# Graph attention layer on one core: the first stage's engine queues and transfers in another order

## The reference, cut to what matters

```python
h0 = maximum(layernorm(x), 0)
h  = h0 @ W.T + b_W
e  = (h @ a1)[:, None] + (h @ a2)[None, :] + b_a       # 4096 x 4096
e  = where(e > 0, e, 0.2 * e)
attention = softmax(where(adj > 0, e, -9e15), axis=1)
out = x + attention @ h
```

## Time and profile before

| | |
|---|---|
| time, median of 3 runs | 202.73 us (201.75 to 202.74) |
| span of the profiled execution, first to last instruction | 200.8 us |
| TensorE (PE) busy | 194.9 us, 97% |
| VectorE (DVE) busy | 183.0 us, 91% |
| ScalarE (ACT) busy | 147.9 us, 74% |
| GpSimd (POOL) busy | 52.4 us, 26% |
| read from memory | 73.08 MB |

### The profile page before, as it was taken

How to read it: one execution, slowest core, us unless ns; L and a number is a source line. 1 busy time by engine, 2 the same in 40 slices (tenths; PEclk the granted TensorE clock), 3 DMA queues, 4 the chain that set the end, 5 groups by cost and what they waited for, 6 DMA issues and landing times.

```text
span 200.8 us, 7230 instructions
## 1 busy us (share of the span) xinstructions
PE 194.9 (97%) x3183; PEld 189.2 (94%) x3183; DVE 183.0 (91%) x265; ACT 147.9 (74%) x192; POOL 52.4 (26%) x66
## 2 busy tenths in 40 slices
PE   7969999999999999999999999999999999999993
PEld 7648889999999999999999999999999999999993
DVE  4779999999998799897999999999999999999745
ACT  2679879898882777689988888899588888996000
POOL 1002479699995010205000000072000000510000
PEclk9999999999999999999999999999999999999999
DMA  5999999999999999999999999999999999997012
GB/s 181 376 417 418 407 403 423 421 418 415 422 432 408 418 423 419 416 421 418 415 419 423 419 418 421 421 411 421 419 418 418 415 421 416 418 383 226 6 43 66
DMA packets 15968, 75.66 MB, mean 377 GB/s; under 512 B 1600, under 2 KB 5952, under 8 KB 7616
## 3 DMA queue, kind: packets, MB, share of 16 engines
q1 hardware_dynamic: 15792, 75.06, 91.7%
q10 hardware_dynamic: 144, 0.13, 0.3%
HBM read 73.08 MB, written 2.11 MB: 374 GB/s over the span
## 4 chain that ended last, share of the span: by engine, by line
PE 91%; DMA 4%; SPq 1%; DVE 1%; issue 1%; POOL 0%
PE ps L836 29%; PE ps L834 29%; PE ps L840 29%; DMA adj_sb<-in_adj_t 4%; PE ps L808 2%; PE ps L798 2%; SPq L268 1%; SPq L273 1%; PE ps L876 1%; DVE mask L476 0%; POOL bad L788 0%; DVE rden L504 0%; DVE rg L510 0%; DVE bad L519 0%; DVE upper L576 0%
## 5 line engine op out<-in xcount | busy, mean ns | idle before, releaser
L834 PE MATMUL ps<-V,w 128*128 128x129 f16 x1024 | 174.3, 221 | 0.0
L836 PE MATMUL ps<-V,w 128*128 128x129 f16 x1024 | 174.3, 221 | 0.0
L840 PE MATMUL ps<-V,w 128*128 128x129 f16 x1024 | 174.3, 221 | 0.0
L379 ACT ACTIVATE mask<-adj_sb 128x1024 bf16<-128x1024 int32 x126 | 125.5, 1056 | 28.6 <-DMA adj_sb<-in_adj_t 28.6
L459 DVE SCALAR_TENSOR_TENSOR w<-g_row,pairs,mask 128x1024 f32<-128x1024 f32 x96 | 120.5, 1320 | 5.5 <-ACT mask L379 3.6
L834 PEld LDWEIGHTS ps<-V,w 128*128 128x128 f16 x1024 | 100.2, 98 | 1.5 <-ACT H L340 0.7
L836 PEld LDWEIGHTS ps<-V,w 128*128 128x128 f16 x1024 | 100.2, 98 | 1.0 <-issue 1.0
L840 PEld LDWEIGHTS ps<-V,w 128*128 128x128 f16 x1024 | 100.2, 98 | 0.0
L459 DVE SCALAR_TENSOR_TENSOR w<-ps,pairs,mask 128x1024 f32<-128x1024 f32 x31 | 37.4, 1267 | 0.0
L785 POOL TENSOR_TENSOR xT<-xT,x_sb 128x512 f32<-128x512 f32 x6 | 11.5, 1932 | 79.8 <-ACT xT L394 79.8
L739 POOL TENSOR_TENSOR x_sb<-x_sb,b_row 128x512 f32<-128x512 f32 x8 | 10.0, 1301 | 0.0
(11 more groups left out here) (93 smaller groups left out, 63.8 us busy)
## 6 DMA issues: line engine op xcount, KB each, us to landing
adj_sb<-in_adj_t SPq DMA_DIRECT2D x64, 1024.0 KB, 10.3
xT<-in_x_t SPq DMA_DIRECT2D x8, 256.0 KB, 7.5
x_sb<-in_x_p SPq DMA_DIRECT2D x3, 512.0 KB, 10.9
g_row<-g_dram SPq DMA_DIRECT2D x1, 1536.0 KB, 10.3
out<-xT SPq DMA_DIRECT2D x3, 512.0 KB, 9.9
x_sb<-in_x_p SPq DMA_DIRECT2D x2, 256.0 KB, 4.2
out<-xT SPq DMA_DIRECT2D x1, 192.0 KB, 3.4
out<-xT SPq DMA_DIRECT2D x3, 64.0 KB, 1.6
```

Of the source, the lines that this page charges most:

```text
L379: nc.scalar.activation(mask[:, m % MASKS, r], adj_sb[:, m % HELD, r], ACT.Relu, scale=CONNECTED).then_inc(mask_ready, 1)
L834: nc.tensor.matmul(sums[:, bank, a, :], w16[:, m % SLOTS, col:col + P, 1], V[:, jt, 0, 0:NF], start=(jt == 0 and a == 0), stop=False, skip ...
L836: nc.tensor.matmul(sums[:, bank, a, :], w16[:, m % SLOTS, col:col + P, 1], V[:, jt, 1, 0:NF], start=False, stop=False, skip_group_check=True)
L840: last = nc.tensor.matmul(sums[:, bank, a, :], w16[:, m % SLOTS, col:col + P, 0], V[:, jt, 0, 0:NF], start=False, stop=(jt == NT - 1), ski ...
```

## The change: what it does

- Scores of part 0 come straight from PSUM (`first_scores`), not from `H`; so they don't wait for `take_chunk`, and `take_chunk(0)` and `(1)` wait for them. Chunk 1 of h goes to PSUM banks 4 and 5, and the sum for `norm` to bank 7.
- The table load for the exponential stands ahead of `take_chunk(0)`, not behind `take_chunk(1)`; the two multiplications for `cc` stand behind `h_chunk(1)` and VectorE's `cc` steps behind the maximum of the scores.
- SP loads x's first set ahead of chunk 1 of the transposed x, and the first `adj` pair in two halves, with a semaphore of its own for the first half, ahead of chunks 2 and 3 and of x's third set.
- The low parts of chunk 0 are made by GpSimd (`first_lows`), and both parts of chunk 1 too (`halves(1)`). They stand ahead of `deviations(2, 3)` in its queue. VectorE's `products` and `lows` and ScalarE's `highs(1)` go away.
- On TensorE `h_chunk(2)` stands behind the row vector's transposes, and step 0 (`first_pair`) ahead of `h_chunk(3)` and `centre_chunk(4)`. Step 0 multiplies first what the high parts allow, then the low parts of its first side, then the second side. The chunks that stood behind step m now stand behind step m + 1.
- VectorE does x's third set's statistics in one go, behind step 0.

```diff
-    H_BANK = (1, 4, 1, 4, 4, 4, 4, 4)
+    H_BANK = (1, 4, 4, 4, 4, 4, 4, 4)
...
                 load_xt(0)
+                load_x(0)
                 load_xt(1)
-                load_x(0)
                 load_x(1)
+                sp.dma_start(adj_sb[:, 0, 0:GC], adj_t[0, :, 0:GC]).then_inc(adj_begun, 16)
                 load_xt(2)
+                load_xt(3)
+                sp.dma_start(adj_sb[:, 0, GC:2 * GC], adj_t[0, :, GC:2 * GC]).then_inc(adj_loaded[0], 16)
                 load_x(2)
-                load_xt(3)
-                load_adj(0)
+                load_adj(1)
                 load_xt(4)
-                load_adj(1)
...
                 def take_chunk(c):
                     act.wait_ge(h_done, c + 1)
+                    if c < 2:
+                        act.wait_ge(scores_ready, 1)
...
                 roots_part()
+                nc.scalar.activation(warm[:], zero_col[:], ACT.Exp)
                 take_chunk(0)
+                weights(0)
                 take_chunk(1)
-                nc.scalar.activation(warm[:], zero_col[:], ACT.Exp)
                 relu_chunk(2)
-                weights(0)
-                relu_chunk(3)
                 highs(0)
                 first_mask()
+                relu_chunk(3)
                 take_chunk(2)
                 mask_part(1)
                 take_chunk(3)
                 relu_chunk(4)
-                highs(1)
...
+                def first_scores():
+                    dve.wait_ge(h_done, 2)
+                    dve.wait_ge(std_ready, 2)
+                    for c in range(2):
+                        r = slice(c * CT, (c + 1) * CT)
+                        of = ps[:, H_BANK[c]:H_BANK[c] + 2, 0:2 * (2 + DOUT)].rearrange("p k (a n) -> p k a n", a=2)
+                        by = rstd[:, 1, r].rearrange("p (k a n) -> p k a n", k=2, n=1).to_broadcast([P, 2, 2, 2])
+                        ins = nc.vector.tensor_tensor(st[:, r, :].rearrange("p (k a) n -> p k a n", k=2),
+                                                      of[:, :, :, 0:2], by, ALU.mult)
+                    ins.then_inc(scores_ready, 1)
...
+                step_(nc.vector.tensor_scalar(rstd[:, 2, 0:GI], rstd[:, 1, 0:GI], gg[:, 1:2], None, ALU.mult))
+                inverse_scales(0)
                 early_mask()
                 pack(0)
                 scale_weights(0)
-                products(0)
                 dve.wait_ge(pairs_ready, 1)
                 weigh_first(0)
-                lows(0)
                 weigh_first(1)
                 weigh(0, 1)
-                statistics(2, 5, 8)
+                statistics(2)
                 weigh(1, 0)
                 weigh(1, 1)
-                products(1)
-                lows(1)
                 scores(1)
...
+                def first_lows():
+                    pool.wait_ge(scaled_ready, 1)
+                    pool.wait_ge(ones_ready, 1)
+                    pool.wait_ge(h_ready, 1)
+                    step(nc.gpsimd.tensor_tensor(prod[:, 0, :, :], H[:, 0:CT, H0:HC],
+                                                 evr[:, 0:CT].rearrange("p (n a) -> p n a", a=1).to_broadcast([P, CT, NF]),
+                                                 ALU.mult))
+                    pool.wait_ge(high_ready, 1)
+                    nc.gpsimd.tensor_tensor(V[:, 0:CT, 1, 0:NF], prod[:, 0, :, :], V[:, 0:CT, 0, 0:NF],
+                                            ALU.subtract).then_inc(low_ready, 1)
+                first_lows()
+                halves(1)
                 deviations(2, 3)
                 halves(2)
...
+                def first_pair():
+                    pe.wait_ge(high_ready, 1)
+                    pe.wait_ge(w_begun, 1)
...
+                    pe.wait_ge(low_ready, 1)
...
+                    pe.wait_ge(w_ready, 2)
...
+                h_chunk(2)
+                first_pair()
                 h_chunk(3)
                 centre_chunk(4)
-                pe.wait_ge(h_ready, 3)
-                whole(0)
+                whole(1)
                 h_chunk(4)
                 centre_chunk(5)
-                whole(1)
+                whole(2)
```

More of the change, by code:

```diff
@@ L211, in gat_layer_kernel @@
         ones_ready = sem("ones_ready")
-        product_ready = sem("product_ready")
         high_ready = sem("high_ready")
@@ L555, in statistics, with inverse_scales @@
                     last.then_inc(var_ready, 1)
+                def first_scores():
[8 more added lines that the diff above has]
+                    ins.then_inc(scores_ready, 1)
+                def inverse_scales(part):
+                    r = slice(*PARTS[part])
+                    nc.vector.reciprocal(H[:, r, ONE], rstd[:, 2, r]).then_inc(ones_ready, 1)
                 def scores(part):
@@ L565, in scores @@
                                             ALU.mult).then_inc(scores_ready, 1)
-                    nc.vector.reciprocal(H[:, r, ONE], rstd[:, 2, r]).then_inc(ones_ready, 1)
+                    inverse_scales(part)
                 def pack(part):
@@ L746, in halves @@
                     r = slice(c * CT + k0, c * CT + k1)
-                    part = 1 if c < 4 else 2
+                    part = (0, 0, 1, 1, 2, 2, 2, 2)[c]
                     pool.wait_ge(scaled_ready, part + 1)
@@ L803, in h_chunk @@
                     if c >= 2:
-                        pe.wait_ge(h_ready, c - 1 if c < 4 else c)
+                        pe.wait_ge(h_ready, c)
                     for j in range(CT):
@@ L842, in products @@
                     return last
+                def first_pair():
+                    pe.wait_ge(high_ready, 1)
+                    pe.wait_ge(w_begun, 1)
+                    for k in range(GI):
+                        if k == CT:
+                            pe.wait_ge(w_ready, 1)
+                        bank, a = sums_at(0, k)
+                        nc.tensor.matmul(sums[:, bank, a, :], w16[:, 0, k * P:(k + 1) * P, 1], V[:, 0, 0, 0:NF],
+                                         start=(a == 0), stop=False, skip_group_check=True)
+                        nc.tensor.matmul(sums[:, bank, a, :], w16[:, 0, k * P:(k + 1) * P, 0], V[:, 0, 0, 0:NF],
+                                         start=False, stop=False, skip_group_check=True)
+                    pe.wait_ge(low_ready, 1)
+                    for k in range(GI):
+                        bank, a = sums_at(0, k)
+                        nc.tensor.matmul(sums[:, bank, a, :], w16[:, 0, k * P:(k + 1) * P, 1], V[:, 0, 1, 0:NF],
+                                         start=False, stop=False, skip_group_check=True)
+                    pe.wait_ge(w_ready, 2)
+                    for k in range(GI):
+                        bank, a = sums_at(0, k)
+                        high = w16[:, 0, GC + k * P:GC + (k + 1) * P, 1]
+                        low = w16[:, 0, GC + k * P:GC + (k + 1) * P, 0]
+                        nc.tensor.matmul(sums[:, bank, a, :], high, V[:, 1, 0, 0:NF], start=False, stop=False,
+                                         skip_group_check=True)
+                        nc.tensor.matmul(sums[:, bank, a, :], high, V[:, 1, 1, 0:NF], start=False, stop=False,
+                                         skip_group_check=True)
+                        last = nc.tensor.matmul(sums[:, bank, a, :], low, V[:, 1, 0, 0:NF], start=False, stop=False,
+                                                skip_group_check=True)
+                    last.then_inc(mm_done, 1)
                 def whole(m):
@@ L853, in _ @@
                 nc.tensor.matmul(ps[:, 5, 0:2], wp[:, 0:DIN], wp[:, AV:AV + 2], start=True, stop=True).then_inc(wa_done, 1)
-                nc.tensor.matmul(ps[:, 6, 0:2], wp[:, BW:BW + 1].to_broadcast([P, P]), wp[:, AV:AV + 2], start=True,
-                                 stop=True).then_inc(cc_done, 1)
                 pe.wait_ge(centre_ready, 1)
@@ L858, in _ @@
                 pe.wait_ge(squares_ready, 1)
-                nc.tensor.matmul(ps[:, 4, 0:DOUT], ones[:], wsq[:], start=True, stop=True).then_inc(norm_summed, 1)
+                nc.tensor.matmul(ps[:, 7, 0:DOUT], ones[:], wsq[:], start=True, stop=True).then_inc(norm_summed, 1)
                 centre_chunk(1)
+                pe.wait_ge(wa_ready, 1)
                 h_chunk(0)
-                pe.wait_ge(norm_ready, 1)
                 h_chunk(1)
-                centre_chunk(2)
+                nc.tensor.matmul(ps[:, 6, 0:2], wp[:, BW:BW + 1].to_broadcast([P, P]), wp[:, AV:AV + 2], start=True,
+                                 stop=True).then_inc(cc_done, 1)
                 pe.wait_ge(t_limits, 1)
                 nc.tensor.transpose(ps[:, G_BANK + 1, 0:P], tt[:, 0:1].to_broadcast([P, P]), ident[:]).then_inc(t_spread, 1)
+                centre_chunk(2)
                 centre_chunk(3)
-                h_chunk(2)
                 pe.wait_ge(t_bounds, 1)
```

67 lines of the change are left out of this document (21 added, 46 removed).

## The result

The changed kernel takes 205.62 us (median of 4 runs, 204.96 to 206.24) against 202.24 us for the kernel before in the same comparison: a ratio of 1.0165, interval 1.0129 to 1.0202. It is 3.4 us slower, where 0.5 us faster was forecast; the time lies outside the range. The profiled execution took 206.24 us with a span of 204.7 us, against 200.8 us before. In the executions whose span is on record beside the time, the time lies about 1.55 us above it, not 0.9 to 1.9; the forecast's span of 200.3 is thus a time of about 201.9.

The account below looks back on a forecast made before the run. TensorE, 97% busy, was taken as the bound, leaving only its idle time before step 0 to win. Step 2 0.70 us earlier, less 0.23 at step 3, leaves 0.47: 0.5 off 202.73 makes 202.2 us, range 200.9 to 203.4.

Parts of the forecast that it names:

- wait for the second side: Middle of step 0: TensorE issues its first 24 products by 15.53, second side's weights come at 15.94, a 0.41 us wait.
- wait at step 3: Step 3's first weights, behind part 1's exponentials and pack, ready at 28.38, due at 28.15: TensorE waits 0.23 us.
- it lands at about 9: First half of adj's first pair, costed at 1.25 us per 512 KB, lands at about 9, ending the mask's 1.03 us wait.
- I cost that at nothing, because this chain is hidden by the h chunks: Start: x's first set loads one place sooner, so statistics finish earlier; counted as 0 us, hidden by the h chunks.
- Rival (d): Start: adj's half or pushed chunks land too late; beyond half a microsecond counts fully, 1 us makes 202.7; 0.13 with no-gain rival.
- no wait of TensorE from step 5 on: Sign of being right: after a short wait at step 3, TensorE waits for nothing from step 5 on, 0 us.
- The part on the chunks: Steps 0 to 3: h and centring blocks of 1.81 us put step 1 at 19.11, step 2 at 23.63, winning 0.70 us.
- a wait near step 7: Sign of being wrong: TensorE waiting near step 7 or step 27; no size given.
- The terms of the start: Chain before step 0: maximum 9.44, shifts 10.67, pack 11.56, transposes 12.37, step 0 at 14.17, which is 2.7 us earlier.
- Rival (c): GpSimd's low parts and halves run at 1.69 us per instruction, 3.8 us more in all: 205.6 us; chance 0.1.
- The rule that spoke against this: GpSimd at twice VectorE's 0.70 us: first lows and halves 7.0 us, step 2's weights 1.1 late, 203.3 us; chance 0.05.
- rival (a): More won at the start, up to a stop at step 27's weights: at most 0.9 us, 201.8; chance 0.2, half beyond it.

Follow-up runs that it names:

- pair whole: The changed kernel with step 0's first adj pair loaded whole in the place where its first half stood: 204.03 us, ratio 1.0106.
- the last variant: The combined variant with h_chunk(3) put inside step 0, ahead of its second side, on TensorE: 202.59 us, ratio 1.0016.
- second and third experiments: Changed kernel each: transfers in before's order, pair in halves at its old place, 204.82 us; step 6's masks ahead of chunk 7's copy on ScalarE, 203.69 us.
- the repaired variants: The changed kernel with whole first pair and step 6's masks ahead of chunk 7's copy, 203.05 us, and kernels built on it, 202.46 and 202.59 us.
- the combined variant: The changed kernel with both repairs, plus statistics(3) ahead of scores(1) and part 2's pack ahead of evr on VectorE: 202.46 us, ratio 1.0018.
- the two repairs: On the changed kernel: first adj pair loaded whole, 204.03 us alone; step 6's masks ahead of chunk 7's copy, 203.69 us alone; both, 203.05 us.

## Why the prediction was wrong, and where it was right

| step | forecast | after | pair whole |
|---|---|---|---|
| scores' maximum | 9.44 | 10.56 | |
| transposes | 12.37 | 13.53 | 12.52 |
| step 0 | 14.17 | 15.32 | 14.31 |
| wait for the second side | 0.41 | 0.43 | 0.42 |
| wait at step 2 | 0 | 1.07 | 0 |
| wait at step 3 | 0.23 | 0.51 | 0.31 |
| waits at steps 6 and 7 | 0 | 1.83 | 1.82 |
| time | 202.2 | 205.62 | 204.03 |

The late start (1.15) and the waits beyond the forecast (0.02, 1.07, 0.28 and 1.83) add to 4.35 us; the span of after, 204.7, is 4.4 above the forecast's 200.3.

**The step that failed first: "it lands at about 9", and with it the statistics, "I cost that at nothing, because this chain is hidden by the h chunks".** The half was priced at the bulk rate of the stretch from 50 on, 512 KB in 1.25 us. That rate was measured on whole pairs, whose rows lie behind one another. The first halves took 1.8 to 2.9 us from the landing ahead of them in five profiles; whole pairs at the same place in the queue took 2.5 to 3.8 with twice the bytes, and landed at 9.0 to 10.3 against 9.3 to 10.7 for the half alone. So the halving bought nothing. The late half alone cost nothing either, since the mask did not wait for it. The price is paid at x's second set, issued just ahead of the half: in both profiles of the changed kernel it landed at 8.30 and 8.87 (6.2 to 7.4 in all the others), the statistics waited 1.21 and 1.84 us for it, and they were no longer hidden. That the half held the set up is likely but not shown: with the same half behind it, it came on time in two other kernels. Step 2's wait, for `adj`'s third pair, had no place in the prediction, which followed VectorE and GpSimd to that step and not the transfers. Rival (d) had the mechanism and put its price in full on lateness; but it looked at the mask and at chunk 2, and the transfer that came late was one ahead of the half in the queue. With the pair whole the time is 1.6 to 1.9 us less.

**The step that failed second: "no wait of TensorE from step 5 on".** The part on the chunks costed TensorE's own queue to step 3, and followed ScalarE to part 1's exponentials. `h_chunk(7)` was moved by one step like the others, but what is queued behind its reader was not looked up: ScalarE's copy of chunk 7, step 6's masks behind it, VectorE's step 6, scores, pack and step 7 behind those. The prediction named a wait near step 7 among its signs of being wrong, but gave it no price. It is 1.82 to 1.84 us in every kernel with this order, and exchanging two lines takes away 1.29 of it; the rest goes with the order of the pack and `evr`.

**What held.** The terms of the start: with the pair whole, step 0 comes at 14.31, and less the excess of the first centring pair over 1.11 us it is at 14.19 there and 14.06 to 14.20 in four more variants, for a forecast of 14.17 (14.39 in the last variant, where chunk 2 of x came 0.41 us late; 14.35 and 14.40 in the second and third experiments, with the halves). The wait of 0.41 in step 0 was 0.41 to 0.43 wherever step 0 kept its order, but for the second profile of the changed kernel, which had none. Rival (c) is refuted: GpSimd's rows in after have the lengths of before, and its chain, started 1.16 late with the rest, ends 1.37 late; 0.34 of it is a wait for the high parts that the forecast had left out.

```profile
13.54 1.05 POOL L757 TENSOR_TENSOR prod<-H,evr 128x516 f32<-128x516 f32 x1 [12.12 <-DVE evr L603]
14.93 1.14 POOL L761 TENSOR_TENSOR V<-prod,V 128x516 f16<-128x516 f32 x1 [0.34 <-ACT V L373]
```

The rule that spoke against this, the Trainium skill's "GPSIMD Engine Reference", "4.1 Engine selection", calls GpSimd about twice as slow with two inputs; here it is 1.05 to 1.14 us against VectorE's 0.69 to 0.70, 1.5 to 1.6 times, and VectorE gains more by being free than GpSimd loses.

**What stays open.** By their waits the repaired variants should lie below the kernel before: at a first pair of 1.11 us the combined one would have a span of 14.19 + 182.63 + 3.33 (last product to the end) = 200.15, against 200.8. Its median is the same as before's, so 0.6 us of the forecast gain is not seen. The timed executions keep no rows, but their spans are on record: 200.4 to 202.0 for the combined variant, and 200.0 to 201.4, with a median of 200.8, for the kernel before. So before goes 0.8 below a profile with one of the shortest first pairs, and the first pair is not all that varies. The profiles show that TensorE's full rate comes at different times, but not whether the variants get it later more often than before does.

The last variant's rows show another candidate, the stop of rival (a). VectorE, then TensorE, whose product ahead of this one starts at 96.55:

```profile
94.64 1.98 DVE L461 SCALAR_TENSOR_TENSOR w<-g_row,pairs,mask 128x1024 f32<-128x1024 f32 x1 [1.48 <-ACT mask L382]
```

```profile
96.68 0.23 PE L835 MATMUL ps<-V,w 128*128 128x129 f16 x1
```

Step 27's first weights are over at 96.62, and TensorE starts 0.07 behind its place in the queue. In the two profiles of before and in the four variants with the whole pair and GpSimd's low parts these weights are over between 95.59 and 96.62, and TensorE took them at 96.89 in the earlier trace rows. So the stop leaves 0.3 to 1.3 us to be won, not always the 0.9 of rival (a). How much it took from the timed executions is not shown.

Nor is it shown why x's second set came on time in two other kernels with the strided half (6.53 and 6.93), though memory gave only 199 and 209 GB/s there; and the two repairs are not additive (1.9 to 2.2 and 1.6 to 1.9 us alone, 2.6 to 2.9 together).

## What to carry to other kernels

Price a transfer by a row with the same layout in memory and at the same place in the queue, not by the bulk rate of a later stretch, and give it a range where no such row exists: here the first half of a block landed no sooner than the whole block, the second half with the same layout came at the bulk rate, and what lay ahead in the queue could be late too. When an instruction is moved by one step, list what is queued behind each of its readers on their engines, down to the last step that it reaches; here it was the last of the moved chunks, five steps on, that did the damage. Add up start, moved work and waits until they close: here the distance from step 0 to the last product came again to 0.01 us in the two profiles of before and closed within 0.04 in the combined variant, and told at once which profiles differed by the start alone. Hold a profile's span against the spans of the timed executions before a sum starts from it.

## What the runs showed of the hardware

The first centring pair, at 5 us, took between 1.10 and 2.06 us over thirteen profiles of kernels that do the same there, the kernel before with 1.11 and 2.05; a pair takes 1.02 at full rate and 1.91 at a granted clock of 0.50. The views give a granted clock of 1.00 for these first stretches throughout, so in them only the length of an instruction tells. The trace's own first record of the granted clock, 1.00, starts at 4.83 us in the first profile of before and at 9.78 in the second; over the thirteen, the pair took 1.10 to 1.11 where that record starts before 5 us, and 2.05 to 2.06 where it starts after 7. The Trainium skill, "TensorE: Matmul & The Clock Gate", Part 1, says that how many products run at the lower rate at the start varies from run to run, and calls the price under 1% of a span. Here it is up to 1.5 us of 202, within that, and as large as the effects that were to be measured. The first profile of before was all the same a fair base for the sum: its span, 200.8, is the median of the 46 timed executions, and the second, 202.3, lies above all of them.

Idle TensorE in the first stage cost twice: with 1.80 us and with 3.08 us without a product the granted clock went down to 0.50 (1.2 GHz), for 3.4 and about 6.8 us, and products took nearly twice as long (the eight transposes 1.91 to 1.93 us against 1.06). With the 1.17 us of after's first profile it stayed at 1.00.
